# Projection stage of a one-layer language tower: latents between the pairs of products, norm and statistics a quad further ahead

## What is computed

```python
h = _layernorm(h)                                # per token, 128 features
c_q = _rms(h @ W_DQ, q_ln_w)                     # latent of 64
c_kv = _rms(h @ W_DKV, kv_ln_w)                  # latent of 128
q = concat(c_q @ W_UQ, rope(c_q @ W_QR))         # 8 heads of 32 + 32
k = concat(c_kv @ W_UK, rope(h @ W_KR))          # 2 heads of 32 + 32
v = c_kv @ W_UV                                  # 2 heads of 64
q, k = _rms(q, q_head_norm_w), _rms(k, k_head_norm_w)
...                                              # attention, then
out = (attn_out + h @ W_VR) @ W_O
```

## Time and profile before

| | us |
|---|---|
| median of three runs | 1992.67 (1991.5 to 1993.55) |
| the profiled execution | 1995.3, its span 1993.5 |
| `front`: first instruction of its block to the last of DVE | 106.84 to 264.17 |
| mean granted clock of TensorE over the span | 0.951 |

### The profile page before, as it was taken

The page is one execution under the profiler, slowest core; times in us unless marked ns, Lnnn a source line. Parts: engine busy times, 40 slices in busy tenths (PEclk is TensorE's granted clock), DMA queues, the critical chain, the costliest instruction groups (busy, mean ns, idle before and its releaser), DMA issues.

```text
span 1993.5 us, 28866 instructions
## 1 busy us (share of the span) xinstructions
PE 1822.1 (91%) x8486; PEld 1453.5 (73%) x8486; DVE 1778.8 (89%) x2271; ACT 1458.5 (73%) x2615; POOL 721.0 (36%) x471
## 2 busy tenths in 40 slices
PE   5456769997879999999999999999999999999998
PEld 3434546665658888888888888788888888888886
DVE  7639878885669999999999999799999999999997
ACT  2134558886768888888888888688888888888886
POOL 4245346663123333333333333233333333333330
PEclk9967779999569999999999999999999999999999
DMA  7500000000033333333333333233333333333331
GB/s 213 145 26 15 5 1 1 0 0 6 25 132 122 115 131 105 132 113 123 126 111 132 108 129 121 90 130 106 132 109 127 123 114 132 105 132 115 122 120 48
DMA packets 105257, 191.47 MB, mean 96 GB/s; under 512 B 13558, under 2 KB 86246, under 8 KB 88550
## 3 DMA queue, kind: packets, MB, share of 16 engines
q1 hardware_dynamic: 103166, 186.77, 27.5%
q0 software_dynamic: 2048, 4.20, 0.7%
HBM read 179.40 MB, written 11.53 MB: 96 GB/s over the span
## 4 chain that ended last, share of the span: by engine, by line
PE 70%; DVE 0%; issue 0%; ACT 0%; DVEq 0%; ACTq 0%
PE f_ps_h L1895 12%; PE f_ps_h L1896 12%; PE f_ps_h L1897 12%; PE f_ps_y L1906 12%; PE f_ps_y L1908 12%; PE f_ps_y L1907 12%; PE f_ps_y L1921 0%; DVE s_lo L1851 0%; DVE scaled L1845 0%; PE f_ps_h L1932 0%; ACT act_out L1806 0%; DVE h L1869 0%; ACT y_t L1830 0%; DVEq L1727 0%; PE f_ps_h L1877 0%
## 5 line engine op out<-in xcount | busy, mean ns | idle before, releaser
L1806 ACT ACTIVATE act_out<-f_ps_h,b_t 128x512 f32<-128x512 f32 x1024 | 648.8, 685 | 257.5 <-PE f_ps_h L1897 257.5
L1845 DVE TENSOR_TENSOR scaled<-act_out,c_row 128x1024 f32<-128x1024 f32 x512 | 752.9, 1471 | 41.9 <-ACT act_out L1806 41.4
L1851 DVE TENSOR_TENSOR s_lo<-scaled,s_hi 128x1024 fp32r<-128x1024 f32 x512 | 672.4, 1313 | 0.1
L1814 ACT ACTIVATE s_hi<-scaled 128x1024 fp32r<-128x1024 f32 x512 | 541.7, 1058 | 2.3 <-DVE scaled L1845 1.5
L1709 POOL CAST w_hi<-w_raw 128x512 fp32r<-128x512 f32 x128 | 200.2, 1564 | 912.4 <-PE f_ps_y L1908 897.4
L1895 PE MATMUL f_ps_h<-x_hi,w_hi 128*128 x1024 | 399.6, 390 | 2.1 <-DVE h L1869 1.5
L1906 PE MATMUL f_ps_y<-s_hi,w_hi 128*128 128x512 f32 x1024 | 398.7, 389 | 3.0 <-DVE s_lo L1851 3.0
L1896 PE MATMUL f_ps_h<-x_lo,w_hi 128*128 x1024 | 399.0, 390 | 0.0
L1897 PE MATMUL f_ps_h<-x_hi,w_lo 128*128 x1024 | 398.8, 389 | 0.0
L1907 PE MATMUL f_ps_y<-s_lo,w_hi 128*128 128x512 f32 x1024 | 398.4, 389 | 0.0
L1908 PE MATMUL f_ps_y<-s_hi,w_lo 128*128 128x512 f32 x1024 | 398.4, 389 | 0.0
(11 more groups left out here) (218 smaller groups left out, 1608.1 us busy)
## 6 DMA issues: line engine op xcount, KB each, us to landing
c_row<-comb_rows SPq DMA_DIRECT2D x128, 1024.0 KB, 4.9
w_raw<-in_w SPq DMA_DIRECT2D x256, 128.0 KB, 4.4
by_slot<-b_zeros SPq DMA_DIRECT2D x1, 3072.0 KB, 13.3
b_gauss_s<-by_slot SPq DMA_DIRECT2D x12, 256.0 KB, 5.5
mixed_rows<-b_mixed SPq DMA_DIRECT2D x12, 256.0 KB, 2.3
out<-h SPq DMA_DIRECT2D x8, 256.0 KB, 4.8
cent<-in_centers SPq DMA_DIRECT2D x1, 1536.0 KB
neg_prec<-in_logvar SPq DMA_DIRECT2D x1, 1536.0 KB
```

What stands on the lines that cost most here:

```text
L1806: last = act.activation(act_out[:, r % 2, c, :], ps_h[:, r % 2, c, :], ACT.Gelu, bias=b1_t[:, c, bass.ds(e, 1)])
L1814: act.activation(s_hi[:, r % RING], scaled[:, r % RING], ACT.Copy).then_inc(hi_ready, 1)
L1845: dve.tensor_tensor(scaled[:, r % RING], act_out[:, r % 2], c_row[:, k, g * GT:(g + 1) * GT].unsqueeze(1).broadcast_to([P, HC, GT]), ALU.m ...
L1851: dve.tensor_tensor(s_lo[:, r % RING], scaled[:, r % RING], s_hi[:, r % RING].bitcast(F32), ALU.subtract).then_inc(lo_ready, 1)
```

## The change

In the loop of each engine the calls stand in another order, and some work on a later quad:

- PE: `turn_x(0)` is made ahead of the loop. In an iteration `latents(s)` come between `pair(first)` and `pair(first + 2)`, `sums(s)` after them, and then `turn_x(s + 1)`.
- ACT: `norm_x(s + 1)` moves to the head of the iteration, ahead of the first `copy_tile`. `copy_c(s)` comes between the two pairs of `copy_tile`. Then come `root_x(s + 2)` (was `s + 1`), `root_kv(s)`, `copy_x(s + 1)` and `root_heads(s - 2)`.
- DVE: `statistics` and `deviations` work on quad `s + 2` (was `s + 1`), with quads 0 and 1 ahead of the loop. `sum_up(first - 1)` and `head_means(s - 2)` move from before the second pair of `rotate` to after `deviations`. `sum_up(first + 1)` moves behind `latent_rms`. `latent_means` also waits for `head_means` of the quad whose `eps_q` it overwrites (`hs_ready`).

No instruction is added to or taken from the program but that wait. The squares of the heads are made by GpSimd before and after.

```diff
--- before.py
+++ after.py
@@ -900,17 +900,19 @@
             act.activation(warm[:], wsum[:, 0:1], ACT.Sqrt)
             root_x(0)
             norm_x(0)
+            copy_x(0)
+            root_x(1)
             for s in range(QUADS + 2):
                 first = (s - 1) * QUAD
+                norm_x(s + 1)
                 copy_tile(first)
                 copy_tile(first + 1)
-                copy_x(s)
-                root_x(s + 1)
+                copy_c(s)
                 copy_tile(first + 2)
                 copy_tile(first + 3)
-                copy_c(s)
-                norm_x(s + 1)
+                root_x(s + 2)
                 root_kv(s)
+                copy_x(s + 1)
                 root_heads(s - 2)
 
         @block.vector
@@ -940,6 +942,7 @@
 
             def latent_means(q):
                 if in_range(q, QUADS):
+                    after(dve, hs_ready, q - 1)
                     dve.wait_ge(ss_ready, q + 1)
                     dve.tensor_scalar(eps_q[:, q % 2], ps_cqs[:, SS_Q:SS_Q + QUAD], RMS_EPS / LQ, RMS_EPS * RMS_EPS,
                                       ALU.mult, ALU.add)
@@ -1006,21 +1009,23 @@
             dve.tensor_copy(w["latent"][:, C_RES:C_COLS], ps_rkv[:, 0, 0:DIM]).then_inc(w_ready, 1)
             statistics(0)
             deviations(0)
+            statistics(1)
+            deviations(1)
             for s in range(QUADS + 2):
                 first = (s - 1) * QUAD
                 rotate(first)
                 rotate(first + 1)
-                statistics(s + 1)
+                statistics(s + 2)
                 sum_up(first - 2)
+                rotate(first + 2)
+                rotate(first + 3)
+                deviations(s + 2)
                 sum_up(first - 1)
                 head_means(s - 2)
-                rotate(first + 2)
-                rotate(first + 3)
-                deviations(s + 1)
                 sum_up(first)
-                sum_up(first + 1)
                 latent_means(s)
                 latent_rms(s)
+                sum_up(first + 1)
                 head_rms(s - 2)
             settle()
 
@@ -1085,13 +1090,14 @@
                         pe.matmul(ps_rkv[:, slot, RES_COLS:RES_COLS + KV_COLS], ckv_t[:, b, at], w["kv"][:],
                                   start=True, stop=True).then_inc(products, 1)
 
+            turn_x(0)
             for s in range(QUADS + 1):
                 first = (s - 1) * QUAD
                 pair(first)
-                turn_x(s)
+                latents(s)
                 pair(first + 2)
-                latents(s)
                 sums(s)
+                turn_x(s + 1)
 
 
 def attend(nc, h, ident, causal, w_out, k_scale, qk, v_all, rms, mv):
```

## The result

The changed kernel takes a median of 1983.7 us (1982.4 to 1985.7, 5 runs) where the kernel before took 1992.1 beside it (1991.5 to 1993.6, 5 runs). The ratio is 0.9954, 95% interval 0.9942 to 0.9965: faster, by a little under half a percent. Two later sets of runs, on two other occasions, each on one chip, gave 0.9965 (0.9951 to 0.9979; 1986.4 against 1992.3) and 0.9976 (0.9965 to 0.9986; 1992.4 against 1997.6). That is 8.4, 5.9 and 5.2 us less, where 5.6 had been forecast.

The account below looks back on a forecast made before the run. VectorE was taken to bound the stage `front`: its iterations sum to 124.16 us, 7.7 less; the fill gives back 1.7 and TensorE 0.4, leaving 5.6 less than the median 1992.67: 1987.1, range 1985.5 to 1996.5.

Parts of the forecast that it names:

- the last one, from the stage to the time: Whole program: the stage's 5.6 us saving was taken off the median 1992.67, giving 1987.1.
- the fill: Stage's start, before the first rotate: that rotate comes at 133.95 in place of 132.27, giving back 1.7 us.
- iteration 7: Light iteration near the stage's end, without statistics, deviations, norm_x or copy_x: forecast 13.10 us.
- ScalarE's waits: Waits of 4.34 and 3.59 us for a VectorE itself at work; removing them was said to give nothing by itself.
- The middle quad: Full quad of the stage, iterations 2 to 5: 16.68 us in place of 17.10, with L938 running free.
- the tail: Quad's end, from the start of L944 to the next rotate: 3.77 us, where it was 2.47.
- The light iterations: Iterations with less work or fewer squares: 1 at 15.86 us, 6 at 13.60, 7 at 13.10, 8 at 14.88.
- third rival: TensorE bounds iterations 1 and 7, each tile first + 2 about 1.6 us late: 1989.9, chance 0.10.
- the amount taken off for TensorE: 0.4 us deducted from the stage's 6.0 us saving for late TensorE products, leaving 5.6.
- first rival: head_means blocked by GpSimd's square in seven quads, 1.07 us each, 7.5 in all: 1994.6, chance 0.35.
- fourth rival: The order does nothing: VectorE's work stays the same and the blocks only move; 1992.7, chance 0.07.
- second rival: GpSimd's gathers come late for statistics; if four quads were late by 3 us, 1993.9; chance 0.03.

Follow-up runs that it names:

- e4: Changed kernel with sum_up(first - 1) and head_means put back before the second pair of rotate: 1988.6 us, ratio to the kernel before 0.9979.
- e5: Changed kernel with ScalarE's norm_x(s + 1) moved from the iteration's head to behind copy_tile(first + 3): 1984.2 us, ratio to the kernel before 0.9930.
- e9: Changed kernel, unchanged, run again on the third chip as the standard there: 1992.4 us.
- e1: Kernel before, unchanged, run and profiled a second time: 1992.95 us, ratio 1.0002.
- e2: Changed kernel, unchanged, run and profiled a second time: 1986.4 us, ratio to the kernel before 0.9965.
- e10: Changed kernel with three small memsets ahead of L987 in head_means, so it starts after the square: 1999.7 us, ratio to the kernel before 1.0010.
- e8: Changed kernel with each sum_up directly behind a rotate, and norm_x and copy_x ahead of root_kv on ScalarE: 1979.3 us, ratio to the kernel before 0.9907.
- e6: Kernel before with ScalarE's root_x(s + 1) moved behind copy_c(s): 1992.9 us, ratio 0.9979.
- e3: Kernel before with sum_up(first - 1) and head_means moved behind deviations, plus the hs_ready wait: 1995.0 us, ratio 1.0009.
- e7: Kernel before with root_x behind copy_c, and sum_up(first - 1) with head_means behind deviations: 1989.3 us, ratio 0.9965.
- e12: Same kernel as e8, run again on the chip of e9: 1979.3 us, ratio to the kernel before 0.9906.

## Why the prediction was right or wrong

The step that failed is the last one, from the stage to the time: the sum was made of the stage alone, and the rest of the program went in at no change and with no allowance in the range. The stage became 6.5 us shorter where 5.6 had been forecast, which by itself, from 1992.1, gives 1985.6 and stays in the range. The other 1.9 of the 8.4 us between the medians came from outside the stage. Inside it two terms were mis-sized, the fill (1.7 us given back, 0.15 measured) and iteration 7 (13.10, 14.70 measured), and one reading was wrong, that of ScalarE's waits. Part by part:

- **The middle quad: right for the new order.** 16.68 forecast, 16.55 measured, with the steps where they were put: L940 at 0.16 in iterations 2 to 5 and still 1.23 in iteration 1, the tail 3.69 for 3.77. e4 shows that the moved sum is what frees L940, and e5 that `norm_x` is what lengthens the tail.
- **The light iterations: right but for one.** Iterations 1, 6 and 8 took 15.71, 13.65 and 15.01 for 15.86, 13.60 and 14.88. Iteration 7 took 14.70 for 13.10, because its third `rotate` waited 1.49 for `v_all`. That is half of the third rival. In e9 only 0.19 was left of it, and TensorE's clock makes the difference: L1058 starts 1.17 us before the iteration's first `rotate` in both, but took 0.65 at a granted clock of 1.00 in e9 and 1.12 at 0.50 here, so L1060 stood 0.5 us earlier, and the first L1088 behind it took 0.59 at 1.00 and 1.01 at 0.50.
- **The fill: a term that was mis-sized.** "The fill gives some back: the first `rotate` comes at … 133.95 in place of 132.27", 1.7 us. From the stage's start it came 0.15 later. I had taken the start of L944, 130.29, as fixed, but in the profile before it is a late one: L1064 had ended at 127.14. In e1 L944 starts 0.04 after the sums, in the first profile after and in e2 as well, in e9 4.3 after. Late against late the price is 26.78 − 25.40 = 1.4, on time against on time 25.6 − 25.0 = 0.6; 0.15 is what comes of a late start before and one on time after. This and iteration 7 cancel in the sum, which is luck: stage 6.5 shorter, forecast 5.6 (6.0 before the amount taken off for TensorE).
- **The first rival: false here, by a tie.** L987 takes 0.16 or 0.17 in all eight places, and in the seven that have a square it starts with it to the hundredth. The square takes 1.27 or 1.28 there and 1.25 elsewhere, so it is the square that gives way a little. e10 moves L987 behind the square's start: 7.7 us more in the stage, and 2.1 above before, where the rival had +1.9. So the doubt was well placed: a delay of 0.02 us in one start takes the whole gain. ("1997.8" for the first and third rival together counts the 0.4 for TensorE twice; it should be 1997.4.) The Trainium skill ("SBUF — State Buffer", Who interferes with whom) has the rule that e10 shows: a `tensor_scalar` that runs in a two-port mode contends with GpSimd, and the one that comes first keeps the shared ports for its whole instruction. Two rows do not fit it: in e5 and e8 a two-input instruction starts 0.39 and 0.03 us before a square by the records, and is held by it all the same.
- **"ScalarE's large waits … taking them away gives nothing by itself": wrong.** e6 takes away the one before L851 and the stage is 3.1 us shorter. The wait was for a VectorE at work, but the second pair of copies, `copy_c`, `sums` and the next products stood behind it, and that chain was as long as VectorE's. This did not spoil the number, since the old quad's length went in as measured. It did hide why the change works: e3, the block alone, gives nothing. What makes it pay is in the rest of the change. e7 shows that `root_x` behind `copy_c` is enough for that; the new order of TensorE and the quad's lead of `statistics` were not tested apart. The fourth rival ("the order does nothing") is what e3 measured, for another reason than it gave, since the block was gone and not moved; it is false for the whole change.
- **The second rival: false.** `statistics` (L927) never waits for a gather after the fill.
- **The range: too narrow below, and that is why the time fell out.** The lower end stood 1.6 under the forecast, and the prediction names nothing in it for the rest of the program. Of the 9.6 us between the two profiled spans 4.3 lie ahead of the stage, and the experts give 1.4 back; in the two later pairs of medians, 5.9 and 5.2, the forecast of 5.6 is met. These stretches have the same instructions in both kernels, and the first differs by up to 8 us between executions of the same kernel on different chips (102.59 to 110.48). My estimate, from 8.4, 5.9 and 5.2, is that a forecast of a median from one profile needs some 3 us on each side for that. With it the lower end would have been about 1982.5, below the result.

Still open is what makes the stretch ahead of the stage longer or shorter, and what holds L947 back in the fill. No run was made for either. The fourteen profiles show that the two go together: the five profiles that start the stage by 105.4 us, those of the first set and the first one after, have L944 or L947 on time, and the nine that start it at 106.87 or later have it late. Among e1 to e12 both go by the set, and with it by the chip.

## What to carry to other kernels

Where a wait on an engine looks harmless because the engine waited for is busy, look at what stands behind it in that engine's list: if another engine's work hangs on it, there is a second path, and a gain on the first is lost again until both are cut (e3 and e6 alone give 0 and 3.9 us, together 7.5). Look at the other engine's clock there too: of the 3.6 us by which e6 brings the products forward, 2.7 are TensorE at a granted clock of 1.00 in place of 0.50. Put reduces, not two-input or `tensor_scalar` instructions, behind whatever starts a GpSimd elementwise instruction, and do not leave a tie: 0.02 us of delay cost 1.1 us seven times. And keep work that is needed a quad later out of the stretch in which an engine is last; `norm_x` there cost 7 us, though the same engine had just idled for 7.03 in one quad.

## What the runs showed of the hardware

- A `tensor_scalar` on 8 elements, with one SBUF input, is held by a GpSimd `tensor_tensor` of 640 elements for all of its 1.25 us when it starts 0.02 after it (e10), and takes 0.17 when the two start together (the square then takes 1.27 or 1.28).
- In e5 L978, with two SBUF inputs, started 0.39 us before a square (196.97 and 197.36), while a gather of GpSimd was running (196.40, 0.95 long), and took 2.02 us, to 0.36 after the square's end. In e8 L973 started 0.03 before a square (195.78 and 195.81), just as a gather ended, and took 1.48 for 0.32, to 0.19 after the square's end. So a two-input instruction can lose to a square that starts behind it by the records. GpSimd's gathers alone lengthened such rows by 0.04 at most where I looked (L977 at 161.11 after the change, 0.52 for 0.48). It was not tested apart.
- A wait can end 3 to 4 us after the last instruction that should end it: L944 or L947 3.1 us late in the profile before, 4.3 in e9, 0.04 in three others of the same two programs (e1, after, e2). In all nine late profiles it starts 23.1 to 23.5 us after the stage's start. The profile puts the late ones down to "remote". What it is was not tested.
- The kernel before has medians of 1992.3, 1996.8 and 1997.6 us on the three chips, and the profiled kernels start the stage at 103.8 to 105.4 us on the first of them and at 107.4 to 110.5 on the other two.
- TensorE at either level, in one program: L1083's four matmuls of 512 columns take 2.08 at 0.50 of the full clock and 1.13 at full. In e3 the two stand in one quad: 2.08 at 192.01, 2.65 us after a wait of 5.00 us had ended, and 1.13 at 197.40, when TensorE had worked nearly without pause since 189.36.
